# Two stages of a vision tower: products of the experts in another order, and spread and residual of the last part as transposes

## The reference

```python
# experts: a shared one for all tokens, and one of 8 for each token
shared_out = _swiglu(x, shared_gate, shared_up, shared_down)   # silu(x@wg.T) * (x@wu.T) @ wd.T
logits = x @ gate_w.T
top_id = jnp.argmax(logits, axis=-1)
xs = x * sigmoid(max(logits))[:, None]
...                                                            # routed_out: expert top_id of xs
return shared_out + routed_out

# last part: three blocks
h = x
for blk in range(3):
    y = _qlora_linear(h, ...)      # first product (256 x 256)
    y = _layernorm(y, ...)
    y = jax.nn.gelu(y, approximate=False)
    y = _qlora_linear(y, ...)      # second product
    h = y + h                      # residual
```

## Time and profile before

| what | us |
|---|---|
| median of 3 runs | 501.48 (500.61 to 502.25) |
| the profiled execution's own time | 497.64 |
| its span, first to last instruction | 495.8 |
| PE busy, share of the span | 392.2, 79% |
| DVE busy | 310.2, 63% |
| ACT busy | 237.2, 48% |
| GpSimd busy | 152.8, 31% |

### The profile page before, as it was taken

One profiled execution on the slowest core, in us unless ns is written; L12 is line 12 of the kernel. 1 busy time (PEld: TensorE's weight loads), 2 busy tenths in 40 slices (PEclk: granted clock), 3 DMA queues, 4 the chain that ended last, 5 costly groups with the idle time before them and its releaser, 6 DMA issues.

```text
span 495.8 us, 9638 instructions
## 1 busy us (share of the span) xinstructions
PE 392.2 (79%) x3584; PEld 281.9 (57%) x3585; DVE 310.2 (63%) x863; ACT 237.2 (48%) x507; POOL 152.8 (31%) x192
## 2 busy tenths in 40 slices
PE   5798878677688998999988995636981357799997
PEld 4566655566577874444544883222440235699996
DVE  3989878899583621222321267889998978446542
ACT  4345554366655401222221204984694876756561
POOL 4387773699511250000000073530100002214310
PEclk9999999899999999999999996765555558999999
DMA  8961111592007023111110037000000000000002
GB/s 267 383 225 18 20 24 28 225 426 118 3 0 288 27 91 112 33 39 39 42 42 22 21 89 278 1 3 2 0 1 0 5 3 2 0 2 0 1 22 79
DMA packets 18513, 36.95 MB, mean 75 GB/s; under 512 B 2424, under 2 KB 14916, under 8 KB 17060
## 3 DMA queue, kind: packets, MB, share of 16 engines
q1 hardware_dynamic: 17540, 33.85, 19.8%
q0 software_dynamic: 928, 2.49, 1.5%
HBM read 29.19 MB, written 5.90 MB: 71 GB/s over the span
## 4 chain that ended last, share of the span: by engine, by line
PE 44%; DVE 22%; ACT 15%; issue 8%; POOL 7%; DMA 2%; SPq 1%; DVEq 0%; ACTq 0%; POOLq 0%
PE psum L1404 9%; PE psum L1406 5%; PE psum L2580 5%; PE psum L2613 3%; POOL front L1353 2%; POOL expert_rows L1346 2%; PE psum L2619 2%; PE psum L908 2%; PE psum L1444 2%; ACT experts L1883 2%; PE psum L2597 1%; PE psum L1461 1%; PE psum L675 1%; DVE ring L2170 1%; PE psum L654 1%
## 5 line engine op out<-in xcount | busy, mean ns | idle before, releaser
L1404 PE MATMUL psum<-experts,ring 128*64 x128 | 44.7, 492 | 0.6 <-ACT ring L1553 0.6
L1405 PE MATMUL psum<-experts,ring 128*64 128x512 f32 (+1 forms) x128 | 44.7, 493 | 0.0
L1205 DVE TENSOR_TENSOR ring<-ring,psum 128x512 f32<-128x512 f32 x13 | 8.9, 688 | 54.1 <-PE psum L1405 32.6
L1353 POOL DMA_INDIRECT front<-expert_results,slot_of x10 | 9.5, 948 | 106.9 <-DMA expert_results<-ring 104.1
L1444 PE MATMUL psum<-front,shared 128*128 128x256 f32 (+1 forms) x160 | 34.6, 370 | 0.0
L2580 PE MATMUL psum<-experts 128*128 128x256 f32 (+1 forms) x120 | 27.5, 372 | 4.6 <-ACT experts L2643 4.6
L1444 PEld LDWEIGHTS psum<-front,shared 128*128 128x128 f32 x160 | 29.3, 190 | 3.1
L1406 PE MATMUL psum<-experts,ring 128*128 x80 | 28.0, 491 | 1.2 <-issue 1.2
L1404 PEld LDWEIGHTS psum<-experts,ring 128*64 128x64 f32 x128 | 16.2, 136 | 21.1 <-issue 17.6
L654 PE MATMUL psum<-experts,ring 128*128 128x256 f32 x108 | 25.1, 382 | 3.5 <-DVE experts L508 1.5
L2580 PEld LDWEIGHTS psum<-experts 128*128 128x128 f32 x120 | 21.9, 190 | 7.6 <-ACT experts L2643 5.4
(11 more groups left out here) (382 smaller groups left out, 1102.0 us busy)
## 6 DMA issues: line engine op xcount, KB each, us to landing
experts<-in_experts SPq DMA_DIRECT2D x8, 1536.0 KB, 12.7
experts<-in_x SPq DMA_DIRECT2D x9, 384.0 KB, 9.1
expert_rows<-zeros SPq DMA_DIRECT2D x1, 1664.0 KB, 14.3
ring<-expert_rows SPq DMA_DIRECT2D x26, 64.0 KB, 2.2
shared<-in_shared SPq DMA_DIRECT2D x1, 1536.0 KB, 19.0
experts<-in_ffn_q SPq DMA_DIRECT2D x1, 1536.0 KB, 6.3
experts<-in_ffn_s SPq DMA_DIRECT2D x1, 1536.0 KB, 9.7
experts<-in_pos_embed SPq DMA_DIRECT2D x1, 1152.0 KB, 9.6
```

The costliest lines, as they stand in the source:

```text
L1353: nc.gpsimd.indirect_dma_start(moved[0:n, t, :], None, ys_dram, bass.IndirectOffsetOnAxis(ap=slot_of[0:n, t:t + 1], axis=0)).then_inc(rows ...
L1404: nc.tensor.matmul(out[0:HALF, :], rows[:, 0:HALF], slot_w(t, block, k, n), **flags)
L1405: return nc.tensor.matmul(out[HALF:P, :], rows[:, HALF:P], own_w(t, block, k, n), **flags)
```

## The change

Experts: `shared_down` of chunk 1 moves from step 4 to the end of step 5, and that of chunk 2 from step 6 to the same place, into bank 2, ahead of the first two `slot_turned`; DVE adds both in step 5; the first `slot_down`, which uses bank 2, waits for that. `l1_weights_tensor` of a slot moves from the end of its step to the next step, behind the gate product. DVE's sums of rows of chunks 0 and 1 move from step 21 to step 23, ahead of the addition of chunk 4, the other two behind it.

Last part: `spread` becomes two transposes of the broadcast columns. The residual of the last block becomes four transposes a chunk into bank 3 (`rest_turned`, behind `first` of the same chunk), which DVE adds to `h` (`rested`, ahead of `joined`); L2621 goes. The variances keep bank 2 alone. ACT does `entered` ahead of `squared`.

```diff
+        SH_BANK = [3, 3, 2, 3, 3]
@@ moe_vector, step g
+                if g == 2:
+                    shared_added(0)
+                if g == SHARED_EARLY - 1:
+                    shared_added(1)
+                    shared_added(2)
+                if g == GROUPS:
+                    row_sums(dve, step, 0)
+                    row_sums(dve, step, 1)
+                    row_shift(dve, 0)
+                if g > SHARED_EARLY and shared_step(g - 1) is not None and shared_step(g - 1)[1] == 1:
+                    shared_added(shared_step(g - 1)[0])
                 if g == GROUPS:
                     row_sums(dve, step, 2)
-                    row_shift(dve, 0)
                     row_shift(dve, 1)
                     row_sums(dve, step, 3)
-                if g == GROUPS - 2:
-                    row_sums(dve, step, 0)
-                if g >= 1 and shared_step(g - 1) is not None and shared_step(g - 1)[1] == 1:
-                    shared_added(shared_step(g - 1)[0])
-                if g == GROUPS - 2:
-                    row_sums(dve, step, 1)
@@ moe_tensor, slot_down
                 if t >= 1:
                     pe.wait_ge(sl_y_ready.sem, sl_y_ready.done(t - 1))
+                else:
+                    pe.wait_ge(sh_added.sem, sh_added.done(MOE_EARLY - 1))
@@ moe_tensor, shared_down
-                if c >= 1:
+                if c == 0:
+                    pe.wait_ge(out_added.sem, out_added.done(NT - 1))
+                elif c != 2:
                     pe.wait_ge(sh_added.sem, sh_added.done(c - 1))
@@ moe_tensor, step g
                 if before is not None:
+                    l1_weights_tensor(pe, before)
                     slot_hidden_turned(before)
...
-                if g >= 1 and shared_step(g - 1) is not None and shared_step(g - 1)[1] == 1:
+                if g == 2:
+                    shared_down(0)
+                if g > SHARED_EARLY and shared_step(g - 1) is not None and shared_step(g - 1)[1] == 1:
                     shared_down(shared_step(g - 1)[0])
                 if g == SHARED_EARLY - 1:
+                    shared_down(1)
+                    shared_down(2)
                     slot_turned(0)
                     slot_turned(1)
...
-                if slot_step(g) is not None:
-                    l1_weights_tensor(pe, slot_step(g))
@@ ffn_vector
-                dve.wait_ge(ffn_rest_ready.sem, ffn_rest_ready.done(c))
+                dve.wait_ge(ffn_rested.sem, ffn_rested.done(c))
...
+            def rested(n):
+                c = n - 2 * NC
+                dve.wait_ge(ffn_rest_turned.sem, ffn_rest_turned.done(c))
+                dve.wait_ge(ffn_rest_ready.sem, ffn_rest_ready.done(c))
+                y = h[:, 2 * c:2 * c + 2, :]
+                nc.vector.tensor_tensor(y, y, psum[:, REST, :].rearrange("p (u d) -> p u d", u=2), ALU.add).then_inc(ffn_rested.sem, 1)
...
                     normed(i - 2)
+                if 2 * NC <= i < STEPS:
+                    rested(i)
                 if i < STEPS:
                     joined(i)
@@ ffn_tensor
-                if n >= 2:
-                    pe.wait_ge(ffn_var_ready.sem, ffn_var_ready.done(n - 2))
+                if n >= 1:
+                    pe.wait_ge(ffn_var_ready.sem, ffn_var_ready.done(n - 1))
...
-                for u, (_, m) in enumerate(tiles_of_chunk(n % NC)):
-                    mm = nc.tensor.matmul(psum[:, 4 + n % 2, u * P:u * P + m], ffn_rs[:, n % 2, u:u + 1].to_broadcast((P, P)), ident[:, 0:m],
-                                          start=True, stop=True)
+                for u in range(2):
+                    tr = nc.tensor.transpose(psum[:, 4 + n % 2, u * P:(u + 1) * P], ffn_rs[:, n % 2, u:u + 1].to_broadcast((P, P)), ident)
...
+            def rest_turned(n):
+                c = n - 2 * NC
+                if c >= 1:
+                    pe.wait_ge(ffn_rested.sem, ffn_rested.done(c - 1))
+                for u, t in enumerate((2 * c, 2 * c + 1)):
+                    for k in range(KD):
+                        tr = nc.tensor.transpose(psum[:, REST, u * D + k * P:u * D + (k + 1) * P], ffn_xT[:, k, t * P:(t + 1) * P], ident)
+                tr.then_inc(ffn_rest_turned.sem, 1)
...
-                            nc.tensor.matmul(z, g[:, k, u * P:u * P + m], ffn_w[:, 2 * b + 1, k, :], start=(k == 0), stop=False)
-                        for k in range(KD):
-                            mm = nc.tensor.matmul(z[:, k * P:(k + 1) * P], ffn_xT[:, k, t * P:t * P + m], ident, start=False, stop=(k == KD - 1))
+                            mm = nc.tensor.matmul(z, g[:, k, u * P:u * P + m], ffn_w[:, 2 * b + 1, k, :], start=(k == 0), stop=(k == KD - 1))
@@ ffn_scalar
-                if i < STEPS:
-                    squared(i)
                 if i < 4:
                     entered(2 + 2 * i)
                     entered(3 + 2 * i)
+                if i < STEPS:
+                    squared(i)
```

More of the change, by code:

```diff
@@ L1215, in shared_added @@
                     y = h[:, 2 * c:2 * c + 2, :]
-                    nc.vector.tensor_tensor(y, y, psum[:, 3, :].rearrange("p (u d) -> p u d", u=2), ALU.add).then_inc(sh_added.sem, 1)
+                    nc.vector.tensor_tensor(y, y, psum[:, SH_BANK[c], :].rearrange("p (u d) -> p u d", u=2), ALU.add).then_inc(sh_added.sem, 1)
                 else:
@@ L1473, in shared_down @@
                 pe.wait_ge(hidden_done.sem, hidden_done.done(2 * c + 1 if c < MOE_EARLY else SLOT_TILES + 2 * c + 1))
-                if c >= 1:
+                if c == 0:
+                    pe.wait_ge(out_added.sem, out_added.done(NT - 1))
+                elif c != 2:
                     pe.wait_ge(sh_added.sem, sh_added.done(c - 1))
-                else:
-                    pe.wait_ge(out_added.sem, out_added.done(NT - 1))
                 if c == MOE_EARLY:
@@ L1482, in shared_down @@
                     for k in range(KF):
-                        mm = nc.tensor.matmul(psum[0:m, 3, u * D:(u + 1) * D], sh_h[c % 2][:, k, u * P:u * P + m], shared_w(2, k, 0, D),
+                        mm = nc.tensor.matmul(psum[0:m, SH_BANK[c], u * D:(u + 1) * D], sh_h[c % 2][:, k, u * P:u * P + m], shared_w(2, k, 0, D),
                                               start=(k == 0), stop=(k == KF - 1))
@@ L2426, in tower @@
         ffn_rest_ready, ffn_joined = Count("ffn_rest_ready"), Count("ffn_joined")
+        ffn_rest_turned, ffn_rested = Count("ffn_rest_turned", s_shifted, PAIRS), Count("ffn_rested", p_ready, PAIRS)
         out_stored = sem("out_stored")
+        VAR, REST = 2, 3
         def tiles_of_chunk(c):
@@ L2497, in variance @@
                     dve.wait_ge(ffn_rs_ready.sem, ffn_rs_ready.done(n - 2))
-                nc.vector.tensor_scalar(ffn_var[:, n % 2, :], psum[:, 2 + n % 2, 0:2], 1.0 / D, LN_EPS, ALU.mult, ALU.add).then_inc(ffn_var_ready.sem, 1)
+                nc.vector.tensor_scalar(ffn_var[:, n % 2, :], psum[:, VAR, 0:2], 1.0 / D, LN_EPS, ALU.mult, ALU.add).then_inc(ffn_var_ready.sem, 1)
             def joined(n):
@@ L2585, in summed @@
                 pe.wait_ge(ffn_joined.sem, ffn_joined.done(n))
-                if n >= 2:
-                    pe.wait_ge(ffn_var_ready.sem, ffn_var_ready.done(n - 2))
+                if n >= 1:
+                    pe.wait_ge(ffn_var_ready.sem, ffn_var_ready.done(n - 1))
                 for u in range(2):
-                    mm = nc.tensor.matmul(psum[:, 2 + n % 2, u:u + 1], ffn_sq[n % 2][:, 0, u * P:(u + 1) * P], ones[:, 0:1], start=True, stop=True)
+                    mm = nc.tensor.matmul(psum[:, VAR, u:u + 1], ffn_sq[n % 2][:, 0, u * P:(u + 1) * P], ones[:, 0:1], start=True, stop=True)
                 mm.then_inc(ffn_summed.sem, 1)
@@ L2595, in spread @@
                     pe.wait_ge(ffn_normed.sem, ffn_normed.done(n - 2))
-                for u, (_, m) in enumerate(tiles_of_chunk(n % NC)):
-                    mm = nc.tensor.matmul(psum[:, 4 + n % 2, u * P:u * P + m], ffn_rs[:, n % 2, u:u + 1].to_broadcast((P, P)), ident[:, 0:m],
-                                          start=True, stop=True)
-                mm.then_inc(ffn_spread.sem, 1)
+                for u in range(2):
+                    tr = nc.tensor.transpose(psum[:, 4 + n % 2, u * P:(u + 1) * P], ffn_rs[:, n % 2, u:u + 1].to_broadcast((P, P)), ident)
+                tr.then_inc(ffn_spread.sem, 1)
+            def rest_turned(n):
[6 more added lines that the diff above has]
+                tr.then_inc(ffn_rest_turned.sem, 1)
             def second(n):
@@ L2632, in ffn_tensor @@
                     turned(3 + 2 * i)
+                if 2 * NC <= i < STEPS:
+                    rest_turned(i)
                 if 0 <= i - 1 < STEPS:
```

## The result

The changed kernel takes **486.78 us** (median of 4 runs, 484.69 to 488.65), the kernel before 501.05 us in the same comparison (4 runs, 499.25 to 502.25). The ratio is 0.9717 with a 95% interval of 0.9667 to 0.9767: faster by 14.3 us. The forecast was 487.9, the range 484.0 to 492.5.

What follows compares the result with a forecast made beforehand. PE was taken to bound the kernel only where it arrives last, in five places. Terms 1.66 + 5.3 - 1.35 + 4.9 + 3.1 = 13.6 us off the 501.48 median gave 487.9, range 484.0 to 492.5.

Steps and rivals of the forecast that it cites:

- Shared product: Ahead of slot 0 in the experts' stage: chunk 2's shared product goes earlier, slot 1 starts sooner; gain 1.66 us.
- Weights: Experts' slots 9 to 12: turning the attention weights one step later takes away PE's waits on DVE; gain 5.3 us.
- Row sums: Behind the gathers: DVE's sums of rows 0 and 1, now after the last shared hidden product, cost 1.35 us.
- Rival 1: Behind the gathers: the experts' stage's gain is given back, loss 3.75, weights' gain only 3.4; 492.2 us, chance 0.12.
- Entry: Start of the last part: ACT copies rows before squaring, first second product comes sooner; gain 3.6 us, 0.44 from two spreads.
- Steps: Last part up to the last first product: transposed spreads gain 2.2 us over ten steps, the transposed residual loses 0.9.
- rival 4: Transposes cost a product's price and the weights' wait only moves to the next place; no change, 501 us, chance 0.03.
- Rival 3: Last part: ACT or DVE becomes the bound and each step keeps its length; 490.7 us, chance 0.12.
- Tail: Last first product to last addition: gain 3.1 us, 4.1 less on PE, nearly one back in waits on DVE and ACT.
- Rival 2: Last block: transposes replace products, the clock falls to half and the kernel gets slower; 511 us, chance 0.04.

## Why the prediction was right, point by point

**Shared product.** Right in size (1.59 for 1.66) and in the walk: the first slot starts 1.09 behind the second transpose, as was taken from before.

**Weights.** The mechanism is right and the term too small, 5.3 for 5.7. The slot's length of 5.69 was read from one that had just restarted behind a wait; slots that follow each other take 5.61 (5.83 from 264.16 to 269.99, less 0.22 for L1719). Four times 0.08, and 0.10 from the row transposes (0.22 each and not 0.27), less 0.05 for the remaining wait, make the difference.

**Row sums.** A loss, as said, of 1.10 and not 1.35. The last hidden product did come 0.4 earlier (8.41 behind the first gather, 8.83 before), and the sums follow each other at 1.9 as before. On the clock of before (2.06 more) the shift of row 0 starts at 298.77, as it did there, so GpSimd's power does set it. What was too long is the part behind it: chunk 4's additions were to end at 299.66 and sum 2 starts at 299.51, the last sum was to end at 305.4 and the shift behind it starts at 305.19. The walk's own figures also give 1.31 (305.4 less 304.09) where it says 1.35. Rival 1, the gain given back there, fails: the loss is far from 3.75.

**Entry.** The sum is right (3.70 for 3.6) and one attribution wrong: 0.44 was put down to the spreads. The run with ACT's old order shows that they count nothing where ACT sets the pace. The walk itself had followed ACT, and came within 0.1.

**Steps.** The mis-sized term is the spread: 0.22 saved in each step was forecast, 0.28 was measured, since I had left a bubble of 0.09 behind the two transposes and only 0.03 of it is there. Ten of these make 2.8, and a transpose at a product's price (rival 4) is out. With the residual's 0.87, which came out as forecast (0.9), that is 1.93. Rival 3 fails: the stretch follows PE.

**Tail.** 3.13 for 3.1. Undone singly, the spread gives back 0.55 of it and the residual 2.35. The mechanism is right, the tenth is luck: PE's waits on DVE and ACT came out at 0.08 and 0.25, where the walk had 0.26 and 0.45, and the last second-product, which starts at 481.03 behind ACT's last Gelu, took 2.18 to the last addition where 1.90 was walked.

**Clock.** Rival 2 had a rule of the Trainium skill behind it ("TensorE: Matmul & The Clock Gate", "PE-mode transpose"), by which transposes don't bring the full clock. In the last block six transposes stand in each step of 4.08 and the clock is 1.00: here, amid products, the trace doesn't follow the rule.

The median came out 1.1 below the forecast. Of that 0.7 is in the stages: 1.3 more than forecast in the edited ones, less the 0.6 of the unedited one. The remainder, 0.4, is the reference: the kernel before had 501.05 in this comparison and 501.48 in the runs shown. That the stages' 14.3 is also the difference of the medians is in part luck. The code ahead of the slots differed by 5.2 between the two traces, and the medians of the kernel before differ by 3.4 between comparisons, so the 1.5 us that the prediction took for a telling difference was too little.

## What to carry to other kernels

Where one engine is busy from start to start, every instruction of its counts in full, and where it waits for another, a cheaper instruction counts nothing; so ask of each stretch who is last there before an edit is priced. A wait can cost more than the idle time in its row, which counts only from the modelled end of the instruction before (0.16 and 0.10 more at slot 0), and at the weights a second gap of 0.38 to 0.54 came behind it; take an edit's price from start to start, and a period's length from periods without a wait. Copies that another engine waits for go ahead of work that nobody waits for, and a table load belongs into idle time ahead of the chain that needs it.

## What was not expected

Code that no edit touches took up to 7 us more or less ahead of the slots. Between 120 and 146 us the granted clock was 0.87 in this execution of the changed kernel and 1.00 in the one with the old row sums, whose code up to there is the same (columns as above):

```profile
120.00:146.00 26.00, 21.10 (x318) 17.12 (x317) 16.35 (x40) 14.89 (x29) 13.42 (x12) 0.87 0.01 2
```
```profile
120.00:146.00 26.00, 20.06 (x355) 16.20 (x335) 17.98 (x45) 15.43 (x32) 13.81 (x12) 1.00 0.01 2
```

The last scatter is issued at 185.95 in the one and 183.18 in the other; over the twelve traces it went from 180.72 (before, 1.00) to 187.85 (shared product back, 0.89). The four traces with a clock of 1.00 have the four earliest (180.72 to 183.21), the eight with 0.79 to 0.93 lie between 184.12 and 187.85, among these in no order by the clock. PE is busy for only 20 to 22 of the 26 us there. That the clock's falls cause the delay wasn't tested, and what sets them off stays open. Differences of this size are as large as those between the runs of one kernel (483.87 to 489.89), so here stages say more than totals.
